# A four-layer transformer kernel on one core: expert tiles of the first batch started earlier, x loads moved, one bank for the last FFN's products

## The reference

```python
x = x + layernorm(L0_attn(layernorm(x)))   # 16 heads of 8, causal, relative bias from q @ rel_key.T
x = x + layernorm(L0_ffn(layernorm(x)))    # silu(x wg) * (x wu) @ wd, hidden 384, int weights / 127
x = x + layernorm(L1_attn(layernorm(x)))   # quaternion linear maps, q and k normed, full softmax
x = x + layernorm(L1_ffn(layernorm(x)))    # 8 experts, top 2 of a softmax router, hidden 512, gelu
```

## Time and profile before

| | us |
|---|---|
| median of 3 runs | 871.47 (870.83 to 872.36) |
| the profiled execution | 872.1 |
| its span, first to last instruction | 869.9 |
| outside the span | 2.2 |
| PE busy / DVE / ACT / POOL | 736.0 / 419.1 / 501.3 / 180.4 |
| mean granted clock of TensorE | 0.947 |

### The profile page before, as it was taken

One profiled execution on the slowest core, in us unless ns is written; L12 is line 12 of the kernel. 1 busy time (PEld: TensorE's weight loads), 2 busy tenths in 40 slices (PEclk: granted clock), 3 DMA queues, 4 the chain that ended last, 5 costly groups with the idle time before them and its releaser, 6 DMA issues. The chain is left out here.

```text
span 869.9 us, 21028 instructions
## 1 busy us (share of the span) xinstructions
PE 736.0 (85%) x8160; PEld 522.1 (60%) x8160; DVE 419.1 (48%) x1389; ACT 501.3 (58%) x1030; POOL 180.4 (21%) x307
## 2 busy tenths in 40 slices
PE   4779997989779999888989987887786878789994
PEld 3668775768545667665555753455553656467763
DVE  3355426664253464225353566473866646531236
ACT  3456564586557586866658765558454556543231
POOL 7101010000100000010100005132315287036230
PEclk9999998999889999999999999999887999989997
DMA  4610400002400000511000412000511021101010
GB/s 113 204 15 3 152 7 5 5 2 64 126 4 14 17 2 15 149 29 17 4 15 1 127 46 72 19 22 22 165 46 43 26 80 37 33 26 50 19 40 24
DMA packets 72358, 40.43 MB, mean 46 GB/s; under 512 B 42726, under 2 KB 62140, under 8 KB 72132
## 3 DMA queue, kind: packets, MB, share of 16 engines
q1 hardware_dynamic: 70468, 35.81, 15.1%
q0 software_dynamic: 1536, 3.15, 1.2%
q10 hardware_dynamic: 256, 0.13, 0.1%
HBM read 20.98 MB, written 17.96 MB: 45 GB/s over the span
## 5 line engine op out<-in xcount | busy, mean ns | idle before, releaser
L954 ACT ACTIVATE late<-ps,j_bias 128x512 f32<-128x512 f32 x256 | 173.9, 695 | 136.3 <-PE ps L1768 135.4
L1220 DVE TENSOR_REDUCE neg_max<-ps 128x2 f32<-128x32 f32 (+31 forms) x128 | 90.5, 707 | 188.3 <-PE ps L1612 179.7
L1768 PE MATMUL ps<-q_heads,k_parts 128*128 128x512 f32 x256 | 131.6, 531 | 20.8 <-ACT late L954 17.2
L794 ACT ACTIVATE probsT<-ps 128x128 f32<-128x128 f32 (+3 forms) x271 | 102.8, 429 | 76.7 <-PE ps L1627 50.0
L880 ACT ACTIVATE probs<-ps,neg_max 128x16 f32<-128x16 f32 (+31 forms) x256 | 110.5, 494 | 16.7 <-DVE neg_max L1220 16.3
L1627 PE MATMUL ps<-ident,probs 128*128 128x128 f32 x640 | 97.1, 283 | 7.5 <-ACT probs L880 7.5
L664 POOL TENSOR_TENSOR q_wide<-qT,eighth_mask 128x1024 f32<-128x1024 f32 x16 | 31.3, 1954 | 303.2 <-PE ps L1612 175.9
L1627 PEld LDWEIGHTS ps<-ident,probs 128*128 128x128 f32 x640 | 76.8, 144 | 26.7 <-ACT probs L880 10.7
L1768 PEld LDWEIGHTS ps<-q_heads,k_parts 128*128 128x128 f32 x256 | 48.5, 197 | 68.9 <-ACT late L954 46.7
L1783 PE MATMUL ps<-late,v_two 128*9 128x512 f32 x512 | 71.3, 630 | 10.9 <-DVE late L1206 8.7
L1605 PE MATMUL ps<-kT_two,q_wide 64*64 64x262 f32 (+16 forms) x1024 | 74.8, 357 | 4.4 <-ACT probsT L794 2.7
(11 more groups left out here) (271 smaller groups left out, 1166.3 us busy)
## 6 DMA issues: line engine op xcount, KB each, us to landing
k_parts<-k_half SPq DMA_DIRECT2D x16, 256.0 KB, 3.1
q_parts<-q_half SPq DMA_DIRECT2D x16, 256.0 KB, 3.9
k_parts<-k_parts SPq DMA_DIRECT2D x16, 256.0 KB, 3.3
q_heads<-q_parts SPq DMA_DIRECT2D x64, 64.0 KB, 2.2
x_by_expert<-q_heads SPq DMA_DIRECT2D x3, 960.0 KB, 7.7
probsT<-x_by_expert SPq DMA_DIRECT2D x45, 64.0 KB, 1.9
y_by_expert<-probsT SPq DMA_DIRECT2D x45, 64.0 KB, 1.5
q_rel<-q_by_token SPq DMA_DIRECT2D x128, 8.0 KB, 2.4
```

What stands on the lines that cost most here:

```text
L794: return nc.scalar.activation(o, i, ACT.Copy)
L954: nc.scalar.activation(head_probs[:, i % SLOTS, :], ps[:, banks[i % len(banks)], :], ACT.Exp, bias=j_bias[:]).then_inc(e2_ready.sem, 1)
L1220: nc.vector.tensor_reduce(neg_max[:, n % 4, :], ps[:, k:k + OCT, 0:QS * (n + 1)], axis=AXX, op=ALU.max, negate=True).then_inc(max_ready.se ...
L1768: mm(ps[:, banks[i % R], :], k_parts[:, hg, kc * P:(kc + 1) * P], q_heads[:, hg % 2, g, :], start=True, stop=True).then_inc(s2_ready.sem, 1)
```

## The change

Seven things move; the computation is the same.

1. X loads of batches 1 to 3: from the head of SyncE's queue to behind the loads of w1 and w2.
2. F in the first four rounds that have an attention beside it: pieces 5 and 6 (the turn of the normed tokens and its copy) three half steps later. In the fifth round pieces 5 to 24 three later and 25 to 36 one later.
3. S in four pieces instead of two, at 52, 55, 58 and 63 (fifth round: 53, 56, 59, 63): store, wait and first heads, two k loads, the rest.
4. X of batch 0: from half step 30 of the fifth round, every second, to half step 14, every third.
5. N of batch 2 in the sixth round: its second group of pieces from 18 to 32 becomes 21 to 29 and 32 to 37.
6. N of batch 1 starts one half step later.
7. The last FFN's `up` products go through bank 7 as the others do; the bank and semaphores kept apart for them go.

```diff
             if a < B:
-                put(r, 6 + late, "F", f, 7)
+                put(r, 6 + late, "F", f, 5)
+                put(r, 14 + late, "F", f, 2)
...
             else:
-                put(r, 16, "F", f, 20)
-                put(r, 39, "F", f, 12)
+                put(r, 19, "F", f, 20)
+                put(r, 40, "F", f, 12)
...
-            put(r, 52, "S", f, 1)
-            put(r, SL - 1, "S", f, 1)
+            for slot in (52, 55, 58, SL - 1) if a < B else (53, 56, 59, SL - 1):
+                put(r, slot, "S", f, 1)
...
-                put(r, 30, "X", 0, NX, 2)
+                put(r, 14, "X", 0, NX, 3)
...
-                put(r, 18, "N", 2, 15)
+                put(r, 21, "N", 2, 9)
+                put(r, 32, "N", 2, 6)
...
-            for b in range(1, B):
-                sp.dma_start(x_all[:, b, :, :], X[b].rearrange("(t p) e -> p t e", p=P)).then_inc(ld_x, 16)
...
                 sp.dma_start(w2_in[:], w2).then_inc(ld_experts, 16)
+                for b in range(1, B):
+                    sp.dma_start(x_all[:, b, :, :], X[b].rearrange("(t p) e -> p t e", p=P)).then_inc(ld_x, 16)
...
                 sp.wait_ge(k_out.sem, k_out.at(b + 1, 0))
...
+                yield
                 spread_k(b, 1)
                 spread_k(b, 2)
                 yield
...
-                    if b < LAST:
-                        fill("F", b, 9 + 4 * f)
-                        mm(bank7, wuT[:, f * P:(f + 1) * P], xnT[:], start=True, stop=True).then_inc(b7_full, 1)
-                    else:
-                        if f:
-                            pe.wait_ge(up_apart_used, f)
-                        mm(ps[:, UP_APART, :], wuT[:, f * P:(f + 1) * P], xnT[:], start=True, stop=True
-                           ).then_inc(up_apart_ps, 1)
+                    for piece, w in ((7, wgT), (9, wuT)):
+                        fill("F", b, piece + 4 * f)
+                        mm(bank7, w[:, f * P:(f + 1) * P], xnT[:], start=True, stop=True).then_inc(b7_full, 1)
```

More of the change, by code:

```diff
@@ L114, in plan @@
             if q - 1 == 1:
-                put(r, 51, "N", 1, 5)
+                put(r, 52, "N", 1, 5)
                 put(r, 59, "N", 1, 15)
-                put(r, 30, "X", 0, NX, 2)
+                put(r, 14, "X", 0, NX, 3)
             if q - 1 == 2:
                 put(r, 10, "N", 2, 5)
-                put(r, 18, "N", 2, 15)
+                put(r, 21, "N", 2, 9)
+                put(r, 32, "N", 2, 6)
                 put(r, 17, "X", 1, NX, 2)
@@ L145, in plan @@
         yield ("D", LAST)
-    UP_APART = 1
-    def up_apart(stage, b, piece):
-        return stage == "F" and b == LAST and piece in (9, 13, 17)
     TURNS = {"H": (2,), "F": (5, 25), "N": (7,)}
@@ L158, in build_sandwich @@
         met[stage, b] = piece + 1
-        if piece in FILLS.get(stage, ()) and not up_apart(stage, b, piece):
+        if piece in FILLS.get(stage, ()):
             fill_no[stage, b, piece] = len(fill_no)
@@ L394, in build_sandwich @@
         attnT_ready = Signal(sem("attnT_ready"), T)
-        up_apart_ps, up_apart_used = sem("up_apart_ps"), sem("up_apart_used")
         ge_ready = Signal(sem("ge_ready"), FT)
@@ L1254, in ffn @@
                     yield
-                    if b < LAST:
-                        full("F", b, 9 + 4 * f)
-                        nc.vector.scalar_tensor_tensor(out=hid[:, f, :], in0=hid[:, f, :], scalar=0.5,
-                                                       in1=bank7, op0=ALU.mult, op1=ALU.mult).then_inc(b7_free, 1)
-                    else:
-                        dve.wait_ge(b7_free, fill_no["F", b, 7 + 4 * f] + 1)
-                        dve.wait_ge(up_apart_ps, f + 1)
-                        nc.vector.scalar_tensor_tensor(out=hid[:, f, :], in0=hid[:, f, :], scalar=0.5,
-                                                       in1=ps[:, UP_APART, :], op0=ALU.mult, op1=ALU.mult
-                                                       ).then_inc(up_apart_used, 1)
+                    full("F", b, 9 + 4 * f)
+                    nc.vector.scalar_tensor_tensor(out=hid[:, f, :], in0=hid[:, f, :], scalar=0.5,
+                                                   in1=bank7, op0=ALU.mult, op1=ALU.mult).then_inc(b7_free, 1)
                     yield
@@ L1704, in ffn @@
                 for f in range(FT):
-                    fill("F", b, 7 + 4 * f)
-                    mm(bank7, wgT[:, f * P:(f + 1) * P], xnT[:], start=True, stop=True).then_inc(b7_full, 1)
-                    yield
-                    yield
-                    if b < LAST:
-                        fill("F", b, 9 + 4 * f)
-                        mm(bank7, wuT[:, f * P:(f + 1) * P], xnT[:], start=True, stop=True).then_inc(b7_full, 1)
-                    else:
-                        if f:
-                            pe.wait_ge(up_apart_used, f)
-                        mm(ps[:, UP_APART, :], wuT[:, f * P:(f + 1) * P], xnT[:], start=True, stop=True
-                           ).then_inc(up_apart_ps, 1)
-                    yield
-                    yield
+                    for piece, w in ((7, wgT), (9, wuT)):
+                        fill("F", b, piece + 4 * f)
+                        mm(bank7, w[:, f * P:(f + 1) * P], xnT[:], start=True, stop=True).then_inc(b7_full, 1)
+                        yield
+                        yield
                 fill("F", b, 19)
-                if b == LAST:
-                    pe.wait_ge(up_apart_used, FT)
                 for t in range(T):
```

## The result

| | before | changed |
|---|---|---|
| median, us | 871.51 (870.83 to 872.36) | 889.48 (888.43 to 898.54) |
| ratio | 1 | 1.0229 (1.0161 to 1.0296) |
| span of the profiled execution | 869.9 | 887.6 |
| mean granted clock | 0.947 | 0.939 |

What follows compares the result with a forecast made beforehand. TensorE, walking one fixed list with single waits, was taken as the bound. The terms summed to -4.2 us: 872.1 profiled to 867.9, or 867.3 for the median, range 859 to 877.

Steps and rivals of the forecast that it cites:

- N in the sixth round: Sixth round: six transfers ahead of each of two tiles cost +3.5 us; the closed wait at N's turn gives -1.
- one bank: Last FFN, fifth round: up waits for VectorE to read gate, uncovered in one pair of three, +1.2 us (0 to 5.7).
- x loads: SyncE's queue at the start: 768 KB of x loads ahead of `q_rel` delay it by +2.5 us (0 to 3).
- later turns: Rounds two to four: the wait for `xn` goes, but products waiting for maxima are late next, -3 us (-10 to 0).
- first tile's start: Fifth round's beginning: TensorE waits about 7.3 us for VectorE's `b_two` and GpSimd's copies, +2.4 us (0 to +6).
- SyncE's stall: Fifth round's end: the tile-load wait behind k and q's round trip (4.7) and slow clock (2.6) go, -7.3 us.
- tiles every third: Fifth round: one more half step per tile shortens three up-product waits for VectorE, summing to 3.6 us; -2.5 us taken.
- rival (d): Rounds two to four: VectorE has room for the maxima, so later turns gain 10 us, not 3; 860.3 us, chance 0.12.
- rival (c): Last FFN: the one bank leaves all three gate-up pairs uncovered, so no change, 871.8 us; chance 0.12.
- Rival (b): Fifth round: early tiles stall the FFN on ScalarE and VectorE, four tiles costing 12.7 us; 880 us, chance 0.20.

Runs made afterwards that it cites:

- the kernel with the gap of before: Changed kernel with the last FFN's groups at half steps 18 to 37 and 41 to 52, four half steps between them: 885.0 us, ratio 1.0148.
- the square: Fifth-round losses against the kernel before: changed kernel 12.0 us; batch 0's tiles moved back 10.2; last FFN moved back 13.2; both back 4.8 (885.1 us).
- 3.2 for two half steps: Kernel before with normed-token turns later and S in four pieces, plus batch 0's tiles from half step 28 instead of 30: 871.7 us, ratio 0.9988.

## Why the prediction was wrong

It forecast 867.3 us, with 859 to 877 as its range and 0.28 for slower. The time was 889.5, outside. The largest miss is the early tiles beside the moved FFN: the term that was to gain 2.5 us lost 7.2 in its round. Next come N in the sixth round (8.7 for 2.5), the one bank (5.3 for 1.2) and the stall of SyncE (4.2 gained for 7.3). The terms, with what each measured alone:

| term | forecast | measured alone | in the trace |
|---|---|---|---|
| x loads | +2.5 | +3.1 | +3.7 at chunk 126 |
| later turns | -3 | -4.4 | -7.3 at chunk 126 |
| first tile's start | +2.4 | not alone | 6.4 waited instead of 7.3 |
| one bank | +1.2 | +5.3 | +5.4 in the fifth round |
| SyncE's stall | -7.3 | -4.2 | -2.8 in the fifth round |
| tiles every third | -2.5 | not alone | +7.2 with the FFN's place |
| N in the sixth round | +3.5 - 1 | +8.7 | +7.3 in the sixth round |

- **The x loads**: right in place and sign, a little low. The working took only the transfer of 768 KB. In the trace `q_rel`'s blocked issue ends at 40.82 instead of 36.25 us (1.2 of it is the profile's start), and TensorE now waits for two tiles of tokens, not one (2.62 and 1.75).
- **The turns**: right, and low. "The next row waits for the maxima behind the norm" came true in the second round alone (3.41 for 5.14); in the third and fourth nothing took the wait's place. My rival (d) had the mechanism, but took all 10 us.
- **First tile's start**: right in place and size. The up product was put at 547.3 us and ran at 546.84, behind 6.4 us of waits.
- **One bank**: the step that failed is "in two of three pairs a piece of a tile now also lies between and covers it". It covered one pair of three: 2.72 and 1.75 us were waited. With tiles at the old place all three stand open, 1.60, 1.76 and 1.75, near the upper bound of 3 x 1.9. Alone the one bank cost 5.3 us, which is rival (c)'s price. The Trainium skill's rule ("PSUM — Partial Sum Buffer", section "Summary: rules for kernel authors", a different bank for reading while a matmul runs) stood beside that rival, and the run agrees with it. The own bank is one that the tiles use, so an order with tiles beside the FFN has to give it up: these 5.3 us are a price of the early tiles too.
- **SyncE's stall**: right that the load's wait goes, wrong that all of 4.68 and of the slow clock is won. VectorE's copy is late next by 2.21 us.
- **Tiles every third**: the term with the wrong sign, and the largest miss. I priced the wider spacing by the three waits of up products for VectorE (3.6 us), and they did close. But I put two things at nothing that stand in the diff. The last FFN's groups were moved by three and by one, so only two half steps were left for its norm on VectorE instead of four; the kernel with the gap of before lost 4.8 us less in that round. And the tiles now share ScalarE and VectorE with the FFN from its start. Rival (b) named this, with 0.20 and 12.7 us; the square gives 7.2 for tiles and FFN together. But its mechanism is not what the changed trace shows: the waits of 1.37 to 2.61 for `hid` stand with the tiles back at 30 too (1.37 to 2.64) and go with the FFN's place, and no up product of a later tile waited 1 us or more for VectorE in that round. The early tiles' own cost is seen only between kernels: 8.4 us with the FFN at its old place, 1.8 with it at the new one, 3.2 for two half steps. That 880 lies nearer to the time than the forecast is in part luck.
- **The sixth round**: right engine, too low. I took the middle between 0 and 7.5 because GpSimd's ring of four might hide some of it; 7.3 were lost. That this is nearly the upper end is luck: the 7.5 came of two stalls of 5.1 each, while the trace has 1.10 and 4.74 us at the two tiles, and about half of the loss is the clock (last section). The closed wait at the turn (-1) opened at a copy in the same VectorE queue and was worth nothing.

**Do the parts close?** Alone they sum to +3.1 + 5.3 + 8.7 - 6.3 = 10.8 us; the changed kernel without early tiles and the FFN's place is at 11.8 (7.7 to 15.9). So there the sum closes by the ratios, each of which is only good to 2 to 4 us; by the medians it is 9.0 and 12.8. What is left of the whole change is the early tiles with the FFN's place: 1 to 8 us by its two ratios, 4 to 5 by its two medians. That they lose 7.2 in the fifth round is read from one profile of each kernel; how much of it reaches the end isn't shown.

## What to carry to other kernels

When two streams that share in-order engines are laid over each other, price their meeting at every engine, not the wait that disappears: here two half steps more of overlap took back 3 to 5 us of a gain of 6. Look up the distance between each producer's last piece and its consumer in the old and new order, since a table edit that moves two groups by different amounts closes a gap nobody mentions. And where a bound of the sum is a whole row of the trace (a gate read before the next product, six transfers before a copy), take that bound unless a row shows the cover.

## What the runs showed of the hardware

A stretch of waits costs more than its brackets where the clock falls. From chunk 225 to chunk 232 of the sixth round TensorE runs the same 100 products in both kernels. Windows of the kernel before, then of the changed one:

```profile
701.20:719.30 18.10, 13.21 (x100) 10.09 (x92) 7.62 (x20) 8.90 (x17) 15.67 (x29) 1.00 0.22 65
```

```profile
712.50:737.50 25.00, 16.96 (x100) 13.63 (x92) 8.58 (x23) 8.95 (x16) 20.16 (x30) 0.80 0.20 59
724.00:727.00 3.00, 3.00 (x15) 2.91 (x15) 0.00 (x0) 0.60 (x1) 2.39 (x3) 0.50 0.14 46
733.00:737.00 4.00, 4.00 (x18) 3.90 (x19) 0.00 (x0) 0.60 (x1) 3.33 (x6) 0.50 0.08 20
738.00:749.00 11.00, 11.00 (x88) 8.70 (x81) 5.42 (x12) 7.95 (x15) 7.36 (x15) 1.00 0.13 37
```

The changed kernel takes 6.9 us more. Of these 3.15 are idle time (8.04 for 4.89) and 3.75 are the products themselves (16.96 for 13.21), which ran in part at 1.2 GHz. One such part stands behind the wait of 4.74 us, from 733 to 737; the other, from 724 to 727, stands ahead of it, behind waits of 1.09 and 1.10 us. From 738 on the clock was full again. In the kernel before, waits of 2.61, 1.11 and 1.10 us in this stretch left the clock at 1.00. So the slow clock isn't the long wait's alone; what decides it these rows don't show.
